# Attention and routed feed-forward on one core: the value products of a unit's last two key tiles listed together

## What is computed

```python
q, k, v = split(layernorm(x) @ Wqkv)           # 32 query heads, one key head, one value head
scores = einsum('bqhd,bkd->bhqk', q, k) * d ** -0.5
scores = where(k_pos <= q_pos, scores + slopes * (k_pos - q_pos), -1e30)
probs = softmax(scores)
x = x + einsum('bhqk,bkd->bqhd', probs, v).reshape(B, S, H) @ Wo
x = x + (layernorm(x) @ W_base.T + b_base) + routed_low_rank(layernorm(x))
```

## Time and profile before

| | |
|---|---|
| median of 3 runs | 703.57 us (703.44 to 704.35) |
| the profiled execution | 700.96 us, span 699.2 us |
| PE busy | 669.7 us (96%) |
| DVE busy | 557.4 us (80%) |
| ACT busy | 358.6 us (51%) |
| POOL busy | 216.9 us (31%) |

### The profile page before, as it was taken

One profiled execution on the slowest core, in us unless ns is written; L12 is line 12 of the kernel. 1 busy time (PEld: TensorE's weight loads), 2 busy tenths in 40 slices (PEclk: granted clock), 3 DMA queues, 4 the chain that ended last, 5 costly groups with the idle time before them and its releaser, 6 DMA issues.

```text
span 699.2 us, 13261 instructions
## 1 busy us (share of the span) xinstructions
PE 669.7 (96%) x4304; PEld 305.5 (44%) x4304; DVE 557.4 (80%) x1801; ACT 358.6 (51%) x511; POOL 216.9 (31%) x366
## 2 busy tenths in 40 slices
PE   3889999999999999999999999999999999999997
PEld 2434344544344444444443343433433455555553
DVE  5899889887989889898988989899881365666565
ACT  2324647567556676666666666767667411111111
POOL 0035424233332515243352231422432412222220
PEclk9999999999999999999999999999999999999999
DMA  8578108080411443080144744225200189700001
GB/s 253 130 145 137 64 2 136 30 147 28 166 54 51 60 89 108 11 131 34 41 63 94 102 81 77 49 49 94 48 18 33 52 130 170 162 30 30 31 30 60
DMA packets 42951, 56.32 MB, mean 81 GB/s; under 512 B 6648, under 2 KB 26232, under 8 KB 42752
## 3 DMA queue, kind: packets, MB, share of 16 engines
q1 hardware_dynamic: 40296, 51.27, 37.3%
q10 hardware_dynamic: 2592, 4.26, 1.8%
HBM read 35.72 MB, written 19.79 MB: 79 GB/s over the span
## 4 chain that ended last, share of the span: by engine, by line
PE 83%; DVE 10%; DMA 3%; ACT 2%; issue 1%; SPq 1%; POOL 0%; DVEq 0%; ACTq 0%; POOLq 0%
PE psum L780 20%; PE psum L732 18%; PE psum L762 13%; PE psum L808 8%; PE psum L830 7%; PE psum L678 7%; PE psum L759 5%; DVE psum L1145 3%; PE psum L825 2%; PE psum L840 2%; ACT work L965 2%; DMA x_sb<-in_x 1%; DVE negm L1150 1%; PE psum L817 1%; DMA arena<-q_dram 1%
## 5 line engine op out<-in xcount | busy, mean ns | idle before, releaser
L965 ACT ACTIVATE work<-psum 128x1024 f32<-128x1024 f32 (+1 forms) x320 | 289.0, 943 | 127.6 <-PE psum L762 108.5
L1145 DVE CUSTOM_DVE_ANT_0 psum<-psum,future 128x384 f32<-128x384 f32 (+3 forms) x512 | 237.7, 514 | 12.6 <-PE psum L732 10.4
L732 PE MATMUL psum<-k_op,arena 106*128 106x512 bf16 (+3 forms) x768 | 212.4, 328 | 9.6 <-DVE negm L1145 4.3
L1150 DVE TENSOR_REDUCE negm<-psum 128x1 f32<-128x512 f32 x256 | 168.6, 687 | 15.3 <-PE psum L732 10.9
L1318 POOL TENSOR_SCALAR_AFFINE_SELECT work<-work 128x512 f32<-128x512 f32 x128 | 81.2, 634 | 296.2 <-ACT work L965 296.2
L780 PE MATMUL psum<-work,v_op 128*32 128x512 f32 (+3 forms) x1536 | 163.5, 498 | 0.5 <-POOL work L1318 0.4
L762 PE MATMUL psum<-arena,k_op 109*128 109x512 bf16 (+3 forms) x640 | 157.3, 316 | 1.9 <-ACT work L965 0.8
L732 PEld LDWEIGHTS psum<-k_op,arena 106*128 106x128 bf16 x768 | 69.0, 97 | 128.5 <-DVE negm L1145 40.7
L678 PE MATMUL psum<-arena,wqkv_sb 128*128 128x256 f32 (+3 forms) x240 | 84.6, 453 | 1.1 <-ACT arena L887 1.1
L759 PE MATMUL psum<-arena,k_op 116*128 116x128 bf16 x512 | 84.3, 221 | 0.9 <-ACT work L965 0.9
L762 PEld LDWEIGHTS psum<-arena,k_op 109*128 109x128 bf16 x640 | 59.6, 98 | 44.5 <-ACT work L965 15.7
(11 more groups left out here) (86 smaller groups left out, 454.8 us busy)
## 6 DMA issues: line engine op xcount, KB each, us to landing
arena<-q_dram SPq DMA_DIRECT2D x96, 128.0 KB, 5.5
o_dram<-o_sb SPq DMA_DIRECT2D x32, 256.0 KB
q_dram<-arena SPq DMA_DIRECT2D x16, 384.0 KB, 4.4
arena<-o_dram SPq DMA_DIRECT2D x32, 128.0 KB, 4.6
arena<-rcp_dram SPq DMA_DIRECT2D x32, 128.0 KB, 4.9
out<-wqkv_sb ACTq DMA_DIRECT2D x16, 256.0 KB, 2.0
x_sb<-in_x SPq DMA_DIRECT2D x3, 1024.0 KB, 10.0
work<-in_x SPq DMA_DIRECT2D x3, 1024.0 KB, 18.8
```

The costliest lines, as they stand in the source:

```text
L732: last = nc.tensor.matmul(bank[:, a * width:(a + 1) * width], q_op[0:ROW_MAX, bass.ds(col, P)], k_op[0:ROW_MAX, b, k0:k0 + width], start=T ...
L965: nc.scalar.activation(probs[:, n % 4, heads * hp:heads * (hp + 1), 0:w], src, ACT.Exp).then_inc(exp_done, 1)
L1145: last = nc.vector.tensor_tensor_reduce(keys, keys, future[:, CH - width:CH], -1.0, 3e38, ALU.add, ALU.min, negm[:, late, 0, j * QT + t:j ...
L1150: nc.vector.tensor_reduce(dst, psum[:, bank, 0:len(js) * width].rearrange("p (a k) -> p a k", a=len(js)), AX_X, ALU.max, negate=True).then ...
```

## The change

Where the walk comes to the value product of a tile with 256 columns (n = 2 or 10), nothing is listed; where it comes to that with 128 columns (n = 3 or 11), both are listed, one behind the other. All other rules stay, the placing of the slots too.

```diff
@@ -194,7 +194,8 @@
             work.append((UH // HALVES[n] * w, ("scores", k - 1, (n, 0))))
         m, v = (k - 1, n - LAG) if n >= LAG else (k - 2, n - LAG + NTI)
         if 0 <= m < NK:
-            work.append((UH * (CH - TILES[v][2]) + PV_FIXED, ("values", m, v)))
+            for tile in {2 * P: (), P: (v - 1, v)}.get(CH - TILES[v][2], (v,)):
+                work.append((UH * (CH - TILES[tile][2]) + PV_FIXED, ("values", m, tile)))
         if 1 <= k <= NK and HALVES[n] == 2:
             work.append((UH // 2 * w, ("scores", k - 1, (n, 1))))
         if k == NK + 1 and n == LAG - 1:
```

## The result

The changed kernel takes 714.12 us (median of 6 runs, 711.61 to 715.98), the kernel before 703.41 (6 runs, 702.69 to 704.35). The ratio is 1.0163, 95% interval 1.0148 to 1.0178: slower by 1.6%, some 11 us. The forecast was 715.8. The profiled execution of the changed kernel took 714.52 us, its span is 712.8.

A forecast was written before the change was run, and what follows sets the result against it. TensorE was taken as the limit in steps 5 to 10 and 12 to 15; 5.75 + 4.9 + 0.46 + 1.15 + 0.2 - 0.24 = 12.2 us on 703.57 gave 715.8 us, 8-in-10 range 709.5 to 719.6.

The forecast's parts named there:

- What bounds the kernel: In steps 5 to 10 and 12 to 15 TensorE is the limit, so any standstill of it adds to the end.
- step 4: Attention step where VectorE was to cover one standstill; the other, 0.41 us less 0.24 for a joined pair, gave +0.2 us.
- first place: Scores (1,0) wait for the exponential of (0,0): +0.47 us a step in steps 5 to 9, +0.52 in 10 and 12 to 15.
- The switches: Value products side by side save 0.24 us a pair; slots fall between most, so only 3 of 31 pairs are joined.
- The cover: The moved value product had filled TensorE's wait for an exponential; without it TensorE stands still 0.3 to 0.5 us.
- the two named scores: Scores (1,0) and (5,0), which may not start until the exponentials of (0,0) and (4,0) are done.
- second place: Scores (5,0) wait for the exponential of (4,0): +0.68 us a step in steps 5 to 9, +0.46 in 10 to 15.
- The sum: All terms over the whole kernel: 12.2 us added, giving 715.8 us, 1.7% slower; this likeliest case had chance 0.72.
- (a): Only standstills near 0.5 us are felt, or VectorE's free time gives part back at the turns: about 710 us, chance 0.12.
- (b): Late copy of bank 7 delays ScalarE's next exponentials and so TensorE, some 0.3 us more in 22 places: 722 us, chance 0.07.
- (c, d): VectorE holds up the slot ahead, hiding the wait: 702.9 us, chance 0.05; with a standstill also gone 701.3 us, 0.04.
- Draining of the array between modes: Changing tiling mode drains TensorE; if all 31 pairs were joined this would be worth 7.4 us, giving 696.2 us.

## Why the prediction was right

**What bounds the kernel**: right from step 5 on. In steps 5 to 10 and 12 to 15 the idle time of TensorE went to the end in full; the steps there are longer by what the two places were reckoned to lose, to 0.05 us. In step 4 it was wrong: VectorE did not cover the first place (0.48 us longer instead of nothing) and was itself on the path at the second (0.38 shorter instead of 0.2 longer).

**The switches**: right in size (0.245 us a join where the pairs were joined in earnest, in steps 5 to 9) and in number: the slots fell between the pairs, and these kept 0.57 and 0.35 to 0.36 us.

**The cover**: right, and shown from several sides. The standstill is at the two named scores in the trace; each place alone gives its share; shorter exponentials take the loss away and do nothing to the kernel before. Two slots in the interval take it away too, but with joins in the account. The terms: first place 0.47 and 0.52 forecast, 0.48 measured for both; second place 0.68 and 0.46, measured 0.68 and 0.44.

**The sum**: 12.2 us forecast on the profiled execution; 12.05 us longer in steps 1 to 15 and 0.3 shorter behind, so 11.75. What was off is small: step 1 is shorter by 0.36 and step 2 longer by 0.24, where both were put at nothing, and in step 4 two errors cancel. Step 1 gains by the second place: with that alone moved it is 0.67 us shorter, with the first alone 0.04. How it does is open. The medians differ by 10.7 us, 1.5 less than the sum; the start of the program alone varies by more than that.

**The rivals.** Hidden in part (a): excluded by the steps' lengths in every part of steps 5 to 15 but the first place of step 11, which the forecast had left out; before step 5, steps 1 and 4 did give some back. A late copy of bank 7 that spreads (b): the copy does come later and ScalarE waits for it, but from step 5 on no step shows more than the two places' price. That VectorE holds up the slot in front (c, d): not in the changed kernel; it does come true as soon as slots are drawn forward. Draining of the array between modes, the rule of the Trainium skill, page "TensorEngine Tiling (Array Packing)", section "Key Properties": the runs agree with it, 0.245 us for each join in steps 5 to 9, and it was outweighed.

**One sign was misjudged.** ScalarE was to be on the chain for 8 to 12 us more. From the end of step 4 to the end of step 15 alone the chain has 21 exponentials of 1.03 us, 21.6 us, where it had none. Each stands there at its full length, also for the part in which TensorE was at work beside it. So the share of the chain says who was waited for, and not what would be won without the wait: that is the idle time and the restart, together 0.47 to 0.68 us a place.

## What to carry to other kernels

Work that stands between a product and the next use of its banks is cover, whatever it is there for; before moving it, add up what is left in the interval and compare it with the reader's time plus its hand-over. Here 0.65 to 0.7 us was left for an exponential of 1.02 (0.87 at the second place of steps 12 to 15), and each such gap cost the missing time and 0.17 us for the restart. A gain by joining work of one kind (here, value products in column strips) has to be read off the final order, since a rule that places other work by summed cost can put it right back between the two, and the same rule decides how much cover is left.

## What was not expected of the hardware

Half the columns of an exponential (two heads of 256 instead of 512) take 0.61 us against 1.02 to 1.03, so by an estimate from these two rows some 0.2 us of it does not depend on the columns.

The six runs of the changed kernel spread over 4.4 us (711.61 to 715.98). That is no trait of the change: the six of the kernel before beside them spread over 1.7, but 29 later ones over 4.5 (699.92 to 704.38). The turn in step 0 came between 48.05 and 51.12 us in the ten traces of this case, with the same instructions ahead of it. From step 5 on, steps of one kind repeat to 0.01 us in all but a few cases. So where a change of some tenths of a per cent is in question, the length of a step tells more than the total.
